# Score rows of two matmuls handed to TensorE in halves between the exponent rows

## The reference

```
layer 0:  q, k, v = split(x @ w_qkv); 16 heads of 16
          dots = q k^T / 4, causal mask (j > i is -inf)
          out = softmax(dots) v @ w_out + b_out
          x = layernorm(x + out)
          x = layernorm(x + ffn(x))       # ternary weights, silu(up) * gate
layer 1:  q = (x * sigmoid(sum|x|)) Wq; 16 query heads, 4 key/value heads
          qk = q k^T / 4 - slope_h * |i - j|
          qk = -1e9 where |i - j| <= 32 or i < 64 or j < 64
          out = softmax(qk) v @ Wo + bo
          x = layernorm(x + out); x = layernorm(x + ffn(x))
```

## Time and profile before

| | before |
|---|---|
| median of 3 runs | 1106.15 us |
| profiled execution, its own time | 1099.92 us |
| its span | 1098.20 us |
| mean granted TensorE clock | 0.973 of full |
| PE busy | 994.7 us (91%) |
| DVE busy | 697.1 us (63%) |
| ACT busy | 605.9 us (55%) |
| POOL busy | 346.5 us (32%) |

### The profile page before, as it was taken

How to read it: one execution, slowest core, us unless ns; L and a number is a source line. 1 busy time by engine, 2 the same in 40 slices (tenths; PEclk the granted TensorE clock), 3 DMA queues, 4 the chain that set the end, 5 groups by cost and what they waited for, 6 DMA issues and landing times. The chain is left out here.

```text
span 1098.2 us, 17969 instructions
## 1 busy us (share of the span) xinstructions
PE 994.7 (91%) x6546; PEld 517.9 (47%) x6546; DVE 697.1 (63%) x1535; ACT 605.9 (55%) x1204; POOL 346.5 (32%) x414
## 2 busy tenths in 40 slices
PE   6688999999988999877799999999999999899995
PEld 4342333333324788653333343433334344698885
DVE  2877877777735566457787777777777724235322
ACT  4335666676665434333566777777776767323321
POOL 3031312222211434321344353524334252324331
PEclk9898999999999899997899999999999999999999
DMA  7552110112000200024433050303211000000001
GB/s 252 168 172 70 59 43 18 59 58 59 2 1 1 74 15 1 23 90 110 148 94 133 30 162 2 124 4 121 71 54 36 1 2 1 1 1 20 20 1 39
DMA packets 32979, 64.19 MB, mean 58 GB/s; under 512 B 6079, under 2 KB 22351, under 8 KB 30516
## 3 DMA queue, kind: packets, MB, share of 16 engines
q1 hardware_dynamic: 31548, 58.47, 17.3%
q0 software_dynamic: 1072, 3.80, 1.0%
q10 hardware_dynamic: 272, 0.79, 0.2%
HBM read 50.45 MB, written 12.32 MB: 57 GB/s over the span
## 5 line engine op out<-in xcount | busy, mean ns | idle before, releaser
L1005 ACT ACTIVATE prob<-ps 128x512 f32<-128x512 f32 (+6 forms) x896 | 442.7, 537 | 211.4 <-PE ps L1048 203.7
L1048 PE MATMUL ps<-qop,kop 98*128 98x512 bf16 (+15 forms) x1376 | 302.4, 291 | 21.3 <-ACT prob L1005 7.6
L1034 PE MATMUL ps<-kop,qop 96*128 96x512 bf16 (+3 forms) x896 | 255.7, 359 | 33.2 <-DVE maxes L940 26.6
L1048 PEld LDWEIGHTS ps<-qop,kop 107*128 107x128 bf16 (+2 forms) x1376 | 114.4, 98 | 278.2 <-ACT prob L1005 200.7
L1075 PE MATMUL ps<-prob,vst 128*32 128x512 f32 (+4 forms) x1792 | 211.2, 543 | 3.9 <-POOL prob L877 2.6
L940 DVE CUSTOM_DVE_ANT_0 sums<-ps,tri 128x128 bf16<-128x128 f32 (+7 forms) x256 | 183.7, 754 | 43.6 <-PE ps L1034 42.3
L940 DVE CUSTOM_DVE_ANT_0 sums<-ps,table 128x960 bf16<-128x960 f32 x128 | 148.0, 1156 | 80.4 <-PE ps L1034 65.8
L877 POOL TENSOR_TENSOR prob<-prob,keep 128x384 int32<-128x384 int32 (+2 forms) x144 | 122.6, 853 | 220.7 <-ACT prob L1005 218.2
L1466 PE MATMUL ps<-xs,wffn 128*128 128x512 f32 x640 | 157.0, 401 | 3.7 <-PEq L715 2.2
L940 DVE CUSTOM_DVE_ANT_0 tri<-ps,table 128x960 bf16<-128x960 f32 x128 | 147.5, 1152 | 3.6 <-PE ps L1034 3.5
L1466 PEld LDWEIGHTS ps<-xs,wffn 128*128 128x128 f32 x640 | 120.4, 191 | 31.5 <-issue 5.1
(11 more groups left out here) (103 smaller groups left out, 686.4 us busy)
## 6 DMA issues: line engine op xcount, KB each, us to landing
table<-in_table SPq DMA_DIRECT2D x32, 464.0 KB, 5.1
qop<-q_parts SPq DMA_DIRECT2D x96, 128.0 KB, 2.6
kop<-k_parts SPq DMA_DIRECT2D x48, 128.0 KB, 2.6
kop<-k_parts SPq DMA_DIRECT2D x48, 96.0 KB
q_parts<-qop SPq DMA_DIRECT2D x8, 384.0 KB, 2.9
q_parts<-kop SPq DMA_DIRECT2D x8, 384.0 KB, 2.6
x<-in_x SPq DMA_DIRECT2D x4, 512.0 KB, 5.5
out<-x SPq DMA_DIRECT2D x4, 512.0 KB, 2.9
```

The costliest lines, as they stand in the source:

```text
L1005: nc.scalar.activation(prob[0:rows, q % 2, k % HG, lo % CH:lo % CH + hi - lo], ps[0:rows, t_bank(n, k), lo % CH:lo % CH + hi - lo], ACT.Ex ...
L1034: last = nc.tensor.matmul(ps[:, S_BANK + 2 * (k % S_SLOTS) + a // CH, a % CH:a % CH + b - a], qop[0:RD, par, h, i0:i0 + P], kop[0:RD, par, ...
L1048: return nc.tensor.matmul(ps[0:rows, bank, a % CH:a % CH + b - a], lhs, rhs, start=start, stop=True, skip_group_check=True)
```

## The change

The change is in the list that `plan` writes and in how PE takes it. A row of two matmuls becomes two steps: `score`, its first matmul, and `close`, its second, which signals `s_full`. A row of one matmul stays one step, `max`. The steps due in a quad are no longer dealt out evenly: a quarter of them stands behind the first exponent row, three quarters by the second, all by the third, and none behind the fourth (`BEHIND_EXP`). DVE does its reduction at `max` or `close`. PE's wait for the slot is at `max` or `score`.

```diff
+BEHIND_EXP = (0.25, 0.75, 1.0, 1.0)
+
+def score_steps(layer, ks, later):
+    out = []
+    for k in ks:
+        wide = len(cut(*units_of(layer)[k][2:])) == 2
+        out += [("score", k, later), ("close", k, later)] if wide else [("max", k, later)]
+    return out
...
-    stream = [(k, 1) for k in range(lead if group >= 1 else 0, nu)] if group + 1 < N else []
-    stream_next = [(k, 2) for k in range(lead)] if group + 2 < N else []
+    stream = score_steps(layer, range(lead if group >= 1 else 0, nu), 1) if group + 1 < N else []
+    stream_next = score_steps(layer, range(lead), 2) if group + 2 < N else []
...
+        start, start_next = given, given_next
         for h in range(HG):
             steps.append(("exp", HG * n + h, 0))
-            upto = given + -(-(due - given) // (HG - h))
-            steps += [("max", u, later) for u, later in stream[given:upto]]
+            upto = start + round((due - start) * BEHIND_EXP[h])
+            steps += stream[given:upto]
             given = upto
...
+            upto = start_next + round((due_next - start_next) * BEHIND_EXP[h])
+            steps += stream_next[given_next:upto]
...
-                    if what == "max":                     # DVE
+                    if what in ("max", "close"):
...
-            def score(k, par):
+            def score(k, par, piece):
...
-                for a, b in cut(lo, hi):
+                last = None
+                for a, b in cut(lo, hi)[piece:piece + 1]:
...
-                    if what == "max":                     # PE
+                    if what in ("max", "score"):
...
-                        score(k, b).then_inc(s_full, 1)
+                        last = score(k, b, 0)
+                        if what == "max":
+                            last = score(k, b, 1) or last
+                            last.then_inc(s_full, 1)
+                    elif what == "close":
+                        score(k, b, 1).then_inc(s_full, 1)
```

More of the change, by code:

```diff
@@ L140, in plan @@
             steps.append(("parts", 0, 1))
+        start, start_next = given, given_next
         for h in range(HG):
             steps.append(("exp", HG * n + h, 0))
-            upto = given + -(-(due - given) // (HG - h))
-            steps += [("max", u, later) for u, later in stream[given:upto]]
+            upto = start + round((due - start) * BEHIND_EXP[h])
+            steps += stream[given:upto]
             given = upto
-            upto = given_next + -(-(due_next - given_next) // (HG - h))
-            steps += [("max", u, later) for u, later in stream_next[given_next:upto]]
+            upto = start_next + round((due_next - start_next) * BEHIND_EXP[h])
+            steps += stream_next[given_next:upto]
             given_next = upto
```

## The result

The changed kernel takes 1120.62 us (median of 4, 1116.38 to 1126.34) against 1105.2 us before (4, 1101.87 to 1106.32): a ratio of 1.0151 with a 95% interval of 1.0098 to 1.0204. Run again (6 executions against 11 of before) it was 1122.18 to 1102.41, 1.0176 (1.0147 to 1.0204). The forecast was 1118.4, range 1109 to 1125, slower.

What follows compares the result with a forecast made beforehand. PE's queue order and the short buffers (two PSUM banks, two score slots) were taken to set the time. Layer 0 +11.7, layer 1's group 0 +4.5, its groups 1 to 6 -4.0: +12.2 on 1106.15 gives 1118.4 us, range 1109 to 1125.

Steps and rivals of the forecast that it cites:

- The recurrence of layer 1: Layer 1, two-row quads: fourth exponent row (E3) follows ACT's second exponential, at +1.51 instead of +1.60; groups 48.4 us.
- the term -4.0: Layer 1, groups 1 to 6: earlier second exponent row, net -0.66 us a group, -4.0 over six.
- counter-term: Layer 1, quads of 64 key rows: two more weight switches each, 2 quads x 0.22 = 0.44 us lost a group.
- The cover of 0.16 us for the slots: Layer 1, groups 1 to 6: slot free at +0.64, wanted at +0.80; without this cover the gain is gone.
- rival 3: Layer 1: slots bind too, the 4.0 is lost and 0.05 a quad added: +20.7 us, 1127; chance 0.11.
- The chain of layer 0: Layer 0: banks through ACT, slots through DVE, followed over 12 quads; +1.94 us a group, +11.7 in all.
- the wait in the last quad: Layer 0, last quad: PE waits over 1 us for `maxes`, row 9 needing row 7 done.
- the two dear quads: Layer 0, third and last quads: rows 15 and 7 closed late, rows 17 and 9 wait; +1.08 and +0.98 us.
- Rival 1: Earlier exponent rows pay in every quad, closings behind the first cost nothing: -11.1 us, 1095.1; chance 0.11.
- Layer 1's group 0: Six quads lengthen as a row's first matmul (S4) waits for the row closed behind `values` (C2): +4.5 us, bounds 0 to 5.4.
- rival 4: Layer 0's new waits make the clock fall once in each of seven groups: +12 us on top, 1130; chance 0.03.

Runs made afterwards that it cites:

- e1: New order only in layer 1, groups 1 to 6, against the kernel before: 1100.1 us, ratio 0.9956.
- e6: Against the kernel before: halves in groups 1 to 6 of both layers, no row cut by `values`, 64-key-row quads with whole rows: 1096.21 us, ratio 0.9934.
- e2: New order only in layer 0, against the kernel before: 1122.47 us, ratio 1.0153.
- e7: Kernel before with its old order, but rows 15 and 7 of layer 0 groups cut by `values`: 1117.79 us, ratio 1.0131.
- e3: Changed kernel, but no row cut by `values` (a quad's last score takes its close along): 1100.0 us, ratio 0.9965 to the kernel before.
- e5: New order only in layer 1's group 0, against the kernel before: 1108.7 us, ratio 1.0047.

## Why the prediction was right, and where it was short

**The recurrence of layer 1** (E0, exponential, exponential, E3, V) held to 0.02 us: E3 forecast at +1.51, measured +1.49; groups forecast at 48.4, measured 48.35; the term -4.0, measured -3.9 (e1). Its counter-term, two more weight switches in the 64-row quads, was right too: the two quads take 3.25 and 3.47 us for 3.02 and 3.27, +0.23 and +0.20 where 0.22 each was forecast, and e6 got it back. The cover of 0.16 us for the slots held, so rival 3 fell.

**The chain of layer 0** was followed quad by quad, and the quads came out so. For quads 0, 1, 2, 3, 10 and 11 the forecasts come to 2.71, 3.41, 3.17, 2.19, 2.64 and 2.60 us; measured were 2.72, 3.43, 3.21, 2.19, 2.67 and 2.62. The group is +2.10 for +1.94, group 6 about +1.4 for +1.3, group 0 +0.9 for +0.7 in the first pair of profiles (it holds a clock fall in every profile and scatters by 1 us and more), and the term +13.3 (e2) for +11.7. One sign did not come as described: the wait in the last quad was to be over 1 us and is 0.89, though the quad is as long as forecast. The cause named for the two dear quads, a wide row that V cuts while its slot is wanted right after, is shown by e7 (make only it) and e3 (take only it away). Rival 1 needed the slot waits to stay under 1.3 us a group; the two of them alone came to 2.05 (1.16 and 0.89). Its point against itself was the right one: DVE's 8 us of spare time lie where PE stands in V and can give it nothing.

**Layer 1's group 0** was forecast at +4.5 and is +5.2 (e5). The mechanism is the one described, S4 waiting for the row of C2; the size was off mainly in the 512-column quads, 0.74 and 0.79 where I took 0.6, and in the 64-row quad, 1.06 where I took 0.85. That the added switches come on top of the wait there fits their 0.2 us a quad, and was not tried by itself.

**The clock** is what the sum left out. I gave rival 4 a chance of 0.03, since in the trace before the clock stayed at full through layer 0. In the first profiled execution it fell in each of the last three groups, the first time after 7.0 us in which PE was busy 5.54, and these three groups were together 8.6 us longer than three at full clock; over ten executions it is 9.6 us more at half clock than before, times 0.344 = 3.3 us. That is the step between +12.2 forecast and the 15 to 20 us that the medians show: about 2.5 us from terms a little too small, about 3 us from the clock. Rival 4's size, a fall in each of seven groups and +12 us, did not come: the four profiles have three falls, one, one and one. The Trainium skill, in the section that I had cited (TensorE: Matmul & The Clock Gate, A second HAM failure mode: psum-queue depth-cycling), says that short idles between matmul groups that cycle PSUM banks can make the clock oscillate. The traces agree with it in part: the clock fell in groups with waits of 0.89 to 1.22 us and not once they were filled, but it also stayed full in most groups with these waits, and in all groups of before, whose PSUM banks cycle as well. Rival 4 deserved a real chance, and the part of the argument that failed was to take the steady clock of a group whose longest wait is 0.46 us as evidence for one that waits 1.2.

**The number itself was also lucky.** The sum of +12.2 was put on a median of three executions of before, 1106.15 us; 40 others have a mean of 1103.7. Ten executions of the changed kernel have a mean of 1121.6, 18.0 more. So the base was 2.5 us too high and the sum 5.8 too small, and 1118.4 came within 3.3 us of that mean because the two errors partly cancel.

## What to carry to other kernels

In this kernel a buffer slot is held from the first instruction that writes into it, but it starts to be worked off only at the last one. Splitting the work of one slot gained time where both parts stood in the same stretch between two V (0.3 us a group in layer 0, 0.7 in layer 1's middle groups), though not in layer 1's group 0 with its three rows a quad. With V between the parts the slot of row 15 is held 1.8 us longer, and DVE on the other side idles. Of a reordering, write down for each slot the three times (claimed, complete, free) in the new order: here this gave the length of the layer 0 quads to 0.05 us. And where a change adds waits of a microsecond to PE, price a clock fall as well, and compare times at the same time spent at half clock.

## What was not expected of the hardware

- The time at half clock differs between executions of one program by 23 us (before) to 28 us (changed) and explains most of the spread: in 40 executions of before 0.344 us of run time for each microsecond, 0.56 us left over.
- Going from score rows (weights of 128 columns) to exponent rows of 64 and back costs about 0.1 us each way (0.29 to 0.32 us between the starts instead of 0.20); leaving out four such switches gained 0.42 us a group.
- ACT starts a waiting exponential of 448 columns 0.44 us after the one before, which itself lasts 0.54; DVE starts the next reduction of 960 columns 1.08 us after one that lasts 1.16. How early the next operand is there decided whether ACT had this overlap: the two exponentials started 0.54 apart before and 0.44 after the change.
